# Rotary operands of a fused transformer kernel: one projection, and the pairs exchanged by DMA, in place of two projections

## The reference

```python
def _rope(x, sin, cos):
    xe, xo = x[..., ::2], x[..., 1::2]
    re = xe * cos - xo * sin
    ro = xe * sin + xo * cos
    return jnp.stack((re, ro), axis=-1).reshape(x.shape)

def _attn(xq, ctx, wq, wkv, wo, bo):
    q = _heads(xq @ wq)
    k, v = jnp.split(ctx @ wkv, 2, axis=-1)
    q, k = _rope(q, ...), _rope(_heads(k), ...)
    sim = jnp.einsum('bhnd,bhmd->bhnm', q, k) * DH ** (-0.5)
    a = softmax(sim)
    return einsum('bhnm,bhmd->bhnd', a, _heads(v)) ... @ wo + bo
```

## Time and profile before

| what | value |
| --- | --- |
| runs | 6561.1, 6564.27, 6563.81 us; median 6563.81 |
| the profiled execution | 6570.67 us; its span, first to last instruction, 6568.9 us |
| instructions | 122562 |
| granted PE clock, mean | 0.967 of full (2.4 GHz) |
| DMA, one queue from SP | 196.34 MB, 11.8% of 16 engines |

### The profile page before, as it was taken

The page is one execution under the profiler, slowest core; times in us unless marked ns, Lnnn a source line. Parts: engine busy times, 40 slices in busy tenths (PEclk is TensorE's granted clock), DMA queues, the critical chain, the costliest instruction groups (busy, mean ns, idle before and its releaser), DMA issues.

```text
span 6568.9 us, 122562 instructions
## 1 busy us (share of the span) xinstructions
PE 6072.1 (92%) x42376; PEld 3586.6 (55%) x42376; DVE 4851.4 (74%) x9782; ACT 4175.0 (64%) x9228; POOL 2747.1 (42%) x2358
## 2 busy tenths in 40 slices
PE   7999999989899998998989999899898999989988
PEld 5566456654556645664455654566445665456644
DVE  6887776657788777675878877667578886876656
ACT  4556676656655668665765666766575566776656
POOL 3466115751246612564025651266402655126630
PEclk8999999999999999998999999999898999999989
DMA  3111011100111101111011100111001111011100
GB/s 87 36 33 26 22 35 31 28 25 19 48 34 33 27 21 37 30 32 28 13 50 36 33 27 19 38 30 33 23 18 49 31 30 30 16 41 30 28 20 12
DMA packets 347662, 204.18 MB, mean 31 GB/s; under 512 B 165005, under 2 KB 319981, under 8 KB 346926
## 3 DMA queue, kind: packets, MB, share of 16 engines
q1 hardware_dynamic: 347054, 196.34, 11.8%
HBM read 105.18 MB, written 1.05 MB: 16 GB/s over the span
## 4 chain that ended last, share of the span: by engine, by line
PE 73%; DVE 10%; ACT 7%; issue 5%; POOL 4%; SPq 1%; DVEq 0%; DMA 0%; POOLq 0%; ACTq 0%
PE ring L1347 37%; PE o_acc L1347 18%; PE scores L1347 17%; DVE max_part L2097 3%; POOL weight_sum L1309 3%; ACT probs L1782 2%; ACT qop L1636 2%; DVE o_inv L2120 1%; POOL qm L1328 1%; DVE region L2059 1%; DVE qop L2056 1%; ACT qm L1636 1%; DVE ring L2073 1%; PE ring L1451 0%; DVE ring L2076 0%
## 5 line engine op out<-in xcount | busy, mean ns | idle before, releaser
L2097 DVE TENSOR_REDUCE max_part<-ring 128x1 f32<-128x400 f32 (+2 forms) x4608 | 2412.7, 577 | 567.4 <-PE ring L1347 543.8
L1782 ACT ACTIVATE probs<-scores 128x512 f32<-128x512 f32 (+1 forms) x3840 | 2105.9, 599 | 1051.5 <-PE scores L1347 961.8
L1309 POOL TENSOR_TENSOR weight_sum<-weight_sum,probs 128x512 f32<-128x512 f32 (+1 forms) x1408 | 1785.7, 1268 | 201.9 <-ACT probs L1782 66.8
L1347 PE MATMUL o_acc<-probs,region 128*32 128x256 f32 (+2 forms) x13312 | 1348.2, 388 | 11.3 <-ACT probs L1782 6.8
L1636 ACT ACTIVATE region<-ring 64x400 f16<-64x400 f32 (+4 forms) x1744 | 820.4, 480 | 480.6 <-PE ring L1347 291.9
L1309 POOL TENSOR_TENSOR weight_sum<-probs 128x512 f32<-128x512 f32 x256 | 325.4, 1271 | 1619.5 <-PE ring L1347 1194.3
L1347 PEld LDWEIGHTS o_acc<-probs,region 128*32 128x32 f32 (+2 forms) x13312 | 586.0, 122 | 547.0 <-issue 202.4
L1347 PE MATMUL scores<-qop,region 128*128 128x256 f16 (+1 forms) x3328 | 804.1, 274 | 11.3 <-ACT qop L1636 7.8
L1347 PE MATMUL scores<-qop,x_cop 128*128 128x256 f16 (+1 forms) x3328 | 800.1, 273 | 0.0
L1347 PE MATMUL ring<-nk,qm 128*128 128x400 f16 (+2 forms) x2560 | 709.5, 337 | 51.9 <-DVE max_part L2097 19.7
L1347 PE MATMUL scores<-qm,nk 128*128 128x512 f16 (+1 forms) x1920 | 657.3, 389 | 62.1 <-ACT probs L1782 32.0
(11 more groups left out here) (170 smaller groups left out, 7265.9 us busy)
## 6 DMA issues: line engine op xcount, KB each, us to landing
x_cop<-region SPq DMA_DIRECT2D x256, 200.1 KB, 3.1
stage<-in_wide SPq DMA_DIRECT2D x512, 64.0 KB, 2.0
nk<-region SPq DMA_DIRECT2D x192, 100.1 KB, 2.2
stage<-in_wide SPq DMA_DIRECT2D x128, 128.0 KB, 2.6
v_stage<-in_wide SPq DMA_DIRECT2D x256, 64.0 KB, 1.9
wo_stage<-in_wide SPq DMA_DIRECT2D x32, 512.0 KB, 4.0
cop_few<-kop_few SPq DMA_DIRECT2D x256, 32.0 KB, 1.9
ff_w<-in_ff_w SPq DMA_DIRECT2D x24, 256.0 KB, 3.4
```

The costliest lines, as they stand in the source:

```text
L1309: pool.tensor_tensor(total, before, probs[0:rows_, (un.chunk + k) % PROBS, :], ALU.add)\
L1347: return pe.matmul(out, lhs, rhs, start=start, stop=stop, skip_group_check=True)
L1782: act.activation(to, src, ACT.Exp, scale=t.scale).then_inc(exp_done.sem, 1)
L2097: dve.tensor_reduce(dst, src, AX.X, ALU.max).then_inc(*release(one))
```

## The change

Each operand of a rotary attention is projected once. ACT copies the product from the bank to one of four SBUF buffers `raw` (`take_raw`) and releases the bank at once. Two DMAs on SP's queue write it with even and odd partitions exchanged to `swapped` (`swap_pairs`). POOL multiplies `swapped` by the sines (`sines`), DVE `raw` by the cosines (`cosines`), and DVE adds the two into `raw` (`add_sines`). ACT's high parts and DVE's low parts then read `raw` in SBUF where they read the bank. The exchanged weights are no longer loaded. A buffer is taken again once the low parts of the operand four before are made (`low_done`). The planner has these steps with durations of its own, rotary projections are due 6 us earlier (`TURN_TIME`), and a unit of sub-block 1 counts 26 us and not 28.

```diff
@@ class Attention
         def op(o):
-            return [("op", o, r) for r in range(2 if self.rope else 1)]
+            return [("op", o, 0)]
@@ make_order
-            put(at, "job", n, j)
+            put(at - TURN_TIME * (kind == "op" and t.rope), "job", n, j)
@@ Plan.wide_job (assumed durations; op on PE and ACT as before)
+                self.part("ACT", "raw", due, raw[1], 0.13 + w * 0.0009, [pe, *low])
+                self.part("SP", "swap", due, swap[1], 1.4, [raw], 2.4)
+                self.part("DVE", "rope", due, one, 0.1 + w * 0.0011, [swap])
+                self.part("POOL", "sines", due, turn[1], 0.2 + w * 0.0021, [swap])
+                self.part("DVE", "turned", due, add[1], 0.1 + w * 0.0011, [turn, ("DVE", one)])
@@ SBUF
-        raw = sb("raw", [P, 2, BANK])
+        raw = sb("raw", [P, TURNS, ROPE_COLS])
+        swapped = sb("swapped", [P, TURNS, ROPE_COLS])
@@ SP
+            def swap_pairs(n, i):
+                z, w = ROPE_AT[n, i] % TURNS, rope_width(n, i)
+                sp.wait_ge(*taken(("job", n, op_job(UNITS[n].t, i))))
...
+                for k in range(2):
+                    sp.dma_start(swapped[k:P:2, z, 0:w], raw[1 - k:P:2, z, 0:w]).then_inc(swap_in[z].sem, 16)
@@ POOL
+                def sines(n, i):
...
+                    pool.wait_ge(*swap_value(r))
+                    v = swapped[:, r % TURNS, 0:w]
+                    pool.tensor_tensor(v, v, rope_sin[:, a0:a0 + w], ALU.mult).then_inc(sines_done.sem, 1)
@@ PE, before the maxima
-                        pe.wait_ge(*taken(("job", n, op_job(t, k + 1))))
+                        if t.rope:
+                            pe.wait_ge(low_done.sem, low_done.at(n, k + 2))
@@ ACT
+                def take_raw(n, i):
...
+                    if r >= TURNS:
+                        act.wait_ge(*rope_value(low_done, r - TURNS))
...
+                    act.wait_ge(*full(one))
+                    copy(raw[:, r % TURNS, 0:w], ring[:, bank(one), 0:w]).then_inc(*release(one))
@@ DVE
-                    kop, v = kop_of(un), ring[:, bank(made), :]
+                    kop, v = kop_of(un), operand(un, i)
...
-                    if k == 0:
-                        dve.wait_ge(rope_step.sem, rope_step.at(n, 3 * max(i - 1, 0)))
-                        dve.tensor_tensor(products, v, rope_cos[:, a0:a0 + w], ALU.mult).then_inc(*release(one))
-                        return
-                    dve.tensor_tensor(v, v, rope_sin[:, a0:a0 + w], ALU.mult).then_inc(rope_step.sem, 1)
...
-                    dve.tensor_tensor(v, v, products, ALU.add).then_inc(rope_step.sem, 2)
+                def cosines(un, i):
...
+                    dve.wait_ge(*swap_value(r))
+                    v = raw[:, r % TURNS, 0:w]
+                    dve.tensor_tensor(v, v, rope_cos[:, a0:a0 + w], ALU.mult).then_inc(cosines_done.sem, 1)
+                def add_sines(n, i):
...
+                    dve.wait_ge(sines_done.sem, sines_done.at(n, i + 1))
+                    v = raw[:, r % TURNS, 0:w]
+                    dve.tensor_tensor(v, v, swapped[:, r % TURNS, 0:w], ALU.add).then_inc(rope_done.sem, 1)
```

More of the change, by code:

```diff
@@ L195 @@
 PRELUDES = sequence()
+ROPE_OPS = [(un.n, i) for un in UNITS if un.t.rope for i in range(un.t.ops)]
+ROPE_AT = {one: r for r, one in enumerate(ROPE_OPS)}
 CHUNKS = [(un, c) for un in UNITS for c in range(un.t.chunks)]
@@ L309, in place_jobs @@
                 put(at, "job", n, j)
-                put(at + (1.5 if last else 3.0), "scale", n)
+                done["scale"] = max(at + (1.5 if last else 3.0), done.get("scale", at) + 0.0001)
+                put(done["scale"], "scale", n)
                 continue
@@ L369, in holds @@
     kind, i, k = t.jobs[j]
-    if kind == "op" and not (t.rope and k == 0):
+    if kind == "op" and t.rope:
+        return "ACT", ("raw", one[1], i)
+    if kind == "op":
         return "DVE", ("job", one[1], t.jobs.index(("low", i, 0)))
@@ L783 @@
 X_NARROW = X_NV + 2 * MP // 2
+ROPE_COLS = max(w for t in ATTS if t.rope for _, w in t.kc)
 X_COLS = max(X_WIDE, X_NARROW, N_MOD * P)
@@ L849, in build @@
         n_t = sb("n_t", [D, 2, N])
[L851 removed]
+        stage = sb("stage", [P, 2, W_COLS])
         v_stage = sb("v_stage", [P, 2, P])
@@ L1025, in keys_from, with rope_width, rope_value, operand @@
             return (src_t[0:DC] if t.sub == 1 else ctx_t)[:, u % 2, :]
+        def rope_width(n, i):
+            return UNITS[n].t.kc[i - 1][1] if i else N
+        def rope_value(count, r):
+            n, i = ROPE_OPS[r]
+            return count.sem, count.at(n, i + 1)
+        def operand(un, i):
+            if un.t.rope:
+                return raw[:, ROPE_AT[un.n, i] % TURNS, :]
+            return ring[:, bank(("job", un.n, op_job(un.t, i))), :]
+        def swap_value(r):
+            n, i = ROPE_OPS[r]
+            count = swap_in[r % TURNS]
+            return count.sem, count.at(n, 32 * sum(ROPE_AT[n, k] % TURNS == r % TURNS for k in range(i + 1)))
         def kop_of(un):
@@ L1334, in program @@
                         pre(one)
+                    elif one[0] == "sines":
+                        sines(one[1], one[2])
                     elif one[0] == "mask":
@@ L1712, in wide_job @@
                     kind, i, k = t.jobs[j]
-                    if kind not in ("op", "val", "shift") or (kind == "op" and t.rope and k == 0):
+                    if kind not in ("op", "val", "shift"):
                         return
@@ L1725, in wide_job @@
                     if t.rope:
-                        act.wait_ge(rope_step.sem, rope_step.at(n, 3 * i + 3))
+                        if i == 0 and un.wide_at >= 2:
+                            old = wide_before(wide_before(un))
+                            act.wait_ge(scores_full.sem, scores_full.at(old.n, old.t.chunks))
+                            act.sem_inc(waited_act, 1)
+                        act.wait_ge(rope_done.sem, rope_done.at(n, i + 1))
                     else:
                         act.wait_ge(*full(one))
+                    made = operand(un, i)
                     for h in range(2):
@@ L1797, in program @@
                         exps(one[1])
+                    elif one[0] == "raw":
+                        take_raw(one[1], one[2])
                     elif one[0] == "cols":
@@ L2082, in job @@
                     if kind == "op" and t.rope:
-                        turn_pairs(one, un, j, i, k)
+                        cosines(un, i)
                     elif kind == "low":
@@ L2126, in program @@
                         pre(one)
+                    elif one[0] == "turned":
+                        add_sines(one[1], one[2])
                     else:
```

98 lines of the change are left out of this document (59 added, 39 removed).

## The result

The changed kernel takes 6891.24 us (median of 4 runs, 6888.43 to 6893.0), the kernel before 6564.04 in the same session (6561.1 to 6565.6): a ratio of 1.0499, interval 1.048 to 1.0517. It is slower by 327 us; 262 were forecast. The profiled execution took 6891.54 us with a span of 6889.8.

The account below looks back on a forecast made before the run. PE bounded sub-block 1 at 25.9 us a unit, DVE 2.8 behind. DVE's 20.4 us plus 10.5 of waits, taken as 30.0, over 64 units gave +262, others 0: 6826 us, range 6450 to 7080.

Parts of the forecast that it names:

- Slower, at 6826: Whole kernel: 6826 us after 6564, from sub-block 1 growing by 262 us; chance of slower 0.74.
- both ranges: Whole kernel's time: 6640 to 7020 us for the likeliest case, 6450 to 7080 to hold 8 in 10.
- Likeliest case: DVE and POOL by turns at SBUF bound sub-block 1, a unit taking 26.1 to 33 us; 6577 to 7020, chance 0.65.
- the three kinds: DVE's cosines, sums and low parts, 20 instructions a unit of sub-block 1: about 1.0 us mean, minimum the old duration.
- One sign: Profile after, sub-block 1: longest of DVE's cosines, sums and low parts near 1.6 us; reciprocals some 30 us apart.
- The wait per unit: DVE in sub-block 1: 20 two-SBUF-input instructions wait for POOL 10.5 us a unit, 14 of them directly behind another.
- DVE nearly full: Sub-block 1 windows: DVE's 20.4 us work plus 10.5 us waits fill the unit, taken as 30.0 us; PE waits.
- Sub-block 0 and stage starts: Sub-block 0 and uncovered stage beginnings together: zero change, within -56 to +56 us.
- The faster rival: Sub-block 1: DVE's waits under 2.6 us a unit fit its slack, PE stays the bound; 6378 or 6322 us, chance 0.21.
- The lock-step rival: Sub-block 1: late sines stop DVE, held banks stop PE, POOL's sums come later; 36.2 us a unit, 7223 us, chance 0.09.
- The clock: PE with gaps may be granted a lower clock, as 0.91 in sub-block 0's stretch; no separate size given.
- The rule of the Trainium skill: Sub-block 1: two-SBUF-input DVE instructions and SBUF-reading POOL instructions block each other fully; 32.8 us a unit by whole durations.

Follow-up runs that it names:

- Experiment 1: DVE and POOL alone, without the kernel's computation: a two-SBUF-input product takes 0.49 us beside idle POOL, 1.56 beside working POOL, 1.14 with a maximum between.
- short sums: POOL's sums of weights cut to 8 of 512 columns: 6476.28 us on the changed kernel, 6516.8 us on the kernel before.
- short sines: Changed kernel with POOL's sine products cut to 8 of their columns: 6719.38 us, ratio 1.0239.
- experiment 2: Changed kernel with cosine product and sum made in the PSUM bank of `ring` again; single projection, copy, transfer and POOL's sines stay: 6891.74 us.
- experiment 6: Kernel before with only some sub-block 1 operands projected once: two 6608.75 us, one 6616.34, two with POOL's sums on 8 columns 6549.48.

## Why the prediction was right, point by point

- **Slower, at 6826 (measured 6891, inside both ranges).** Likeliest case and mechanism hold: the three kinds with two SBUF inputs are long, their minimum is the old duration or less, the maxima unchanged, PE has gaps of which DVE ends 48 of 79 us, POOL's sums slightly longer (1363 ns in the stretch against 1270). One sign didn't come: the maximum was to be near 1.6 us, one POOL instruction, and is 5.24; and the reciprocals are 30 us apart only on the mean.
- **The wait per unit: forecast 10.5 us, measured 8.2.** Short by reading: 106.8 us of DVE a stretch, in which 13 units' operands stand. The estimate let 14 of 20 wait for nearly a whole POOL instruction. Experiment 1 shows why that is too much: what stands between two such instructions counts against the wait (1.14 in place of 1.56 us).
- **DVE nearly full: wrong.** It is busy for 400 of 454 us, 88%. A period of 30.0 us was forecast, 4.1 more than before; 30.5 was measured, 4.9 more. In the second pair's stretch it is, for each of 15 periods, 19.5 us of DVE's own work, 7.1 of waits and 3.6 idle (293.2, 106.8 and 54.3 us), where the forecast had 20.4 and 10.5, cut to 30.0 in all, and nothing idle. The smaller wait and the idle time cancel: that the total came so near is luck in part. The idle time is the part to learn from. It is 54 to 59 us in after, in short sums and in short sines, and in these three the stretch moves with DVE's busy time almost one for one. An engine that is busy for 84 to 88% can set the pace: what it idles are short waits, most of them for PE's next result (17.5 us before the 400-column maxima alone), which don't go away when its own work grows. The share by itself shows nothing: before, DVE is busy for 85% and idle for 57.6 us too, and there PE had no gap.
- **Sub-block 0 and stage starts: forecast 0, within 56; measured 33** (9 + 24), inside the bound. Of the 65 us between 6826 and 6891, 33 are these, and 32 are sub-block 1 (294 for 262).
- **The faster rival** needed waits under 2.6 us a unit; they are 8.2. But the short sums show that even with most of POOL's work gone the change is worth 40 us, not the 186 that the difference of sub-blocks 1 and 7 promised. The 186 was too much: it takes 2.9 us from middle units, while the whole stretches of the kernel before differ by 35.8 us (384.5 and 348.7), 143 in all. With short sums the four stretches of sub-block 1 gain 34 us (1535.1 to 1501.3), sub-block 0 gains 32, and the ways between the two lose 14. Of the 109 that the stretches lack, some 90 are waits that sines and outputs' products still cause (22.5 us x 4 stretches, if the stretch follows DVE as it did twice). The rest, some 20, and the 14 between the sub-blocks would be the longer way. This split is rough and stays open.
- **The lock-step rival**: its price didn't come, its mechanism did in small: POOL's instructions passing a waiting DVE instruction several times, banks held by late maxima, a lower clock.
- **The clock**: 1.00 to 0.92 in the stretch. PE's busy time with 172 matmul rows fewer is only 5 us less. Against the short sums, with the same products (2404 and 2401 rows) and a clock of 0.98, it is 28.1 us longer (375.6 and 347.5), and its gaps 51.7 us: so up to 28 of the 79.8 us between these stretches may be the clock's, as a consequence of the gaps. No experiment holds the clock fixed, so its share is open.
- **The rule of the Trainium skill** (SBUF — State Buffer, "Who interferes with whom") gave 32.8 us a unit by the prediction's sum, the forecast had 30.0, measured 30.5. Its core, that one SBUF input doesn't contend and two do, is what experiments 1 and 2 show (576 to 580 ns against 876 to 1035).

## What to carry to other kernels

Moving an operand from PSUM to SBUF is not free for DVE when POOL is at work: count the DVE instructions that then read two SBUF inputs, and price each at its own time and up to one POOL instruction, less what stands before it; look also at where they stand, since one of them in front of the copies that the scores need delays all that comes behind it (experiment 6). Leaving it in PSUM only helps if the bank is not held through the longer chain; here both ways came to the same 327 us, for different reasons. When an engine at 85% sits between two others, don't read its idle share as slack, nor as a sign that it sets the pace: test it by shortening its work, and see whether the stage follows.

## What the runs showed of the hardware

- A DVE product with two SBUF inputs is not sure of its turn. In the whole profile after, one cosine product of 401 columns, 0.58 us of work, stood for 5.24 us (the group, then that instruction):

```profile
L2160 DVE TENSOR_TENSOR raw<-raw,rope_cos x448: 354/608/5239, 45.0 to 5808.5; 128x256 f32<-128x256 f32 x64, 128x400 f32<-128x400 f32 x64, 128x401 f32<-128x401 f32 x22
...
L2160 DVE TENSOR_TENSOR raw<-raw,rope_cos x1: 5237/5237/5237, 1966.2 to 1966.2; 128x401 f32<-128x401 f32 x1
```

  In that time POOL ran four sine products in a row (3.33 us from 1966.47 on) and went on with its sums at 1969.77.

- Beside a chain of POOL sums that never waits, the steady state is one for one: 1.56 us for each DVE product, 0.49 alone.
- A DVE instruction that takes one input from PSUM and the other from the tile that POOL has just written in SBUF (L2159 in experiment 2) shows no delay, 580 ns: here it is the number of SBUF inputs and not the tile that counts.
